# Transformer block with two attentions: the output weights and the feed forward's second weights at another place in SBUF, the attended values too

## What is computed

```python
h = layernorm(x, ln1);  x = attention(h, h, sa_wq, sa_wk, sa_wv, sa_wo) + sa_bo + x
h = layernorm(x, ln2);  x = attention(h, ctx, ca_wq, ca_wk, ca_wv, ca_wo) + ca_bo + x
h = layernorm(x, ln3);  p = h @ ff_w1 + ff_b1
a, gate = p[..., :1024], p[..., 1024:]
out = (a * gelu(gate)) @ ff_w2 + ff_b2 + x
```

## The kernel before, in words

| tile | byte | modulo 512 | modulo 1024 |
|---|---|---|---|
| `w_hi`, all four slots | 16512 | 128 | 128 |
| `w_lo`, all four slots | 49280 | 128 | 128 |
| `hT_hi` | 133184 | 64 | 64 |
| `hT_lo` | 137280 | 64 | 64 |
| `qk_hi`, `qk_lo`, `v_f` | 141376, 149568, 157760 | 64 | 64 |
| `pT` | 190720 | 256 | 256 |
| `a_hi` | 207168 | 320 | 320 |
| `a_lo` | 215360 | 320 | 320 |

## Time and profile before

### The profile page before, as it was taken

How to read it: one execution, slowest core, us unless ns; L and a number is a source line. 1 busy time by engine, 2 the same in 40 slices (tenths; PEclk the granted TensorE clock), 3 DMA queues, 4 the chain that set the end, 5 groups by cost and what they waited for, 6 DMA issues and landing times.

```text
span 2864.2 us, 72446 instructions
## 1 busy us (share of the span) xinstructions
PE 2842.0 (99%) x25278; PEld 2485.3 (87%) x25278; DVE 2256.3 (79%) x3495; ACT 1912.3 (67%) x6041; POOL 1471.1 (51%) x1310
## 2 busy tenths in 40 slices
PE   8999999999999999999999999999999999999999
PEld 6888888888888888888888888888888889999999
DVE  6888888888888888888888888888888865555554
ACT  6677766677766776777777777777777754444443
POOL 5444444444444444765555555555555544554554
PEclk9999999999999999999999999999999999999999
DMA  5666666666666666667777776666766632222222
GB/s 147 158 162 157 156 157 159 158 154 145 151 151 154 150 148 149 161 166 177 177 172 169 173 171 169 168 164 165 168 168 163 151 100 88 73 73 84 81 73 63
DMA packets 355360, 413.32 MB, mean 144 GB/s; under 512 B 122048, under 2 KB 209472, under 8 KB 355264
## 3 DMA queue, kind: packets, MB, share of 16 engines
q1 hardware_dynamic: 345120, 395.29, 57.4%
q10 hardware_dynamic: 10144, 16.78, 1.6%
HBM read 94.52 MB, written 49.02 MB: 50 GB/s over the span
## 4 chain that ended last, share of the span: by engine, by line
PE 98%; DVE 1%; ACT 1%; POOL 0%; issue 0%; DMA 0%; DVEq 0%; POOLq 0%; ACTq 0%
PE unit_ps L593 54%; PE o_ps L618 17%; PE s_ps L606 14%; PE s_ps L593 12%; DVE neg_max L1021 0%; ACT probs L851 0%; DVE blocks L1035 0%; POOL probs L1253 0%; DMA x_ln<-in_x_dram 0%; ACT qk_hi L882 0%; DVE qk_lo L1046 0%; DVE hT L1016 0%; DVE hT_lo L1059 0%; ACT x_n L828 0%; ACT L828 0%
## 5 line engine op out<-in xcount | busy, mean ns | idle before, releaser
L1253 POOL TENSOR_TENSOR probs<-probs,row_inv 128x1024 f32<-128x1024 f32 x512 | 967.8, 1896 | 893.9 <-DVE row_inv L1026 893.9
L851 ACT ACTIVATE probs<-s_ps,neg_max 128x256 f32<-128x256 f32 x2048 | 950.4, 487 | 403.9 <-DVE neg_max L1021 403.4
L1021 DVE TENSOR_REDUCE neg_max<-s_ps 128x4 f32<-128x1024 f32 x512 | 616.8, 1205 | 62.8 <-PE s_ps L606 58.4
L1035 DVE STREAM_TRANSPOSE blocks<-probs 128x1024 f32<-128x1024 f32 x512 | 633.2, 1237 | 19.9 <-POOL probs L1253 19.9
L593 PE MATMUL unit_ps<-hT_hi,w_hi 128*128 128x256 f32 x2048 | 571.3, 282 | 3.0 <-DVE hT_lo L1059 2.6
L593 PE MATMUL unit_ps<-hT_hi,w_lo 128*128 128x256 f32 x2048 | 554.0, 277 | 0.0
L618 PE MATMUL o_ps<-pT,v_f 128*64 128x256 f32 x4096 | 498.5, 385 | 1.7 <-DVE a_lo L1041 1.7
L593 PE MATMUL unit_ps<-hT_lo,w_hi 128*128 128x256 f32 x1792 | 496.1, 277 | 0.0
L851 ACT ACTIVATION_READ_ACCUMULATOR probs<-s_ps,neg_max 128x1 f32 x2048 | 444.6, 217 | 0.0
L593 PE MATMUL unit_ps<-w_hi,a_hi 128*128 128x256 f32 x1536 | 430.8, 280 | 3.8 <-DVE a_lo L1041 2.8
L593 PE MATMUL unit_ps<-w_lo,a_hi 128*128 128x256 f32 x1536 | 425.7, 277 | 0.0
(11 more groups left out here) (73 smaller groups left out, 6017.8 us busy)
## 6 DMA issues: line engine op xcount, KB each, us to landing
pT<-blocks SPq DMA_DIRECT2D x1024, 256.0 KB, 4.5
rows_t_dram<-row_blocks SPq DMA_DIRECT2D x91, 256.0 KB, 4.4
rows_in<-rows_t_dram SPq DMA_DIRECT2D x91, 256.0 KB, 4.1
x_res<-in_x_dram SPq DMA_DIRECT2D x32, 256.0 KB, 4.1
x_sa_dram<-x_out SPq DMA_DIRECT2D x32, 256.0 KB, 4.3
x_ln<-x_sa_dram ACTq DMA_DIRECT2D x32, 256.0 KB, 4.9
ctx_in<-in_ctx_dram SPq DMA_DIRECT2D x32, 256.0 KB, 4.4
x_res<-x_sa_dram SPq DMA_DIRECT2D x32, 256.0 KB, 4.1
```

The costliest lines, as they stand in the source:

```text
L851: op = nc.scalar.activation(probs[:, m % 2, r, :].rearrange("p (j b c) -> p j b c", j=IT, c=BLK), scored.rearrange("p (j c b) -> p j b c", ...
L1021: nc.vector.tensor_reduce(neg_max[:, m % RING, :], s_ps[:, m % 2, :, :].rearrange("p h (i j) -> p (h i) j", j=S), AX_X, ALU.max, negate=Tr ...
L1035: nc.vector.transpose(blocks[:, n % 2, :, m % 2, :].rearrange("p b (j r c) -> p r j b c", j=IT, c=BLK), probs[:, m % 2, :, :].rearrange("p ...
L1253: nc.gpsimd.tensor_tensor(probs[:, m % 2, :, :], probs[:, m % 2, :, :], row_inv[:, m % RING, :].unsqueeze(2).broadcast_to([P, ROWS, S]), A ...
```

## The change

The fourth slot of the weights (`streamed`) is put 64 bytes further than its neighbours, and 448 bytes behind it make each of the two weight tiles 33280 bytes long, 65 times 512. The 64 bytes ahead of the attended values go. `ff_w2` now lives in the fourth slot, where `wo` was; its raw form is loaded to slot 2 of the staging as before. Since `wo` is in use to the end of the attention, the split is made in two halves: each half waits until `wo`'s same half is used for the last time (`at.wo_full`).

```diff
+        def weights(name):
+            loaded = sb(f"{name}_loaded", [P, 3, WCOLS], F32R)
+            sb(f"{name}_between", [P, 16])
+            streamed = sb(f"{name}_streamed", [P, WCOLS], F32R)
+            sb(f"{name}_behind", [P, 112])
+            return [loaded[:, i, :] for i in range(3)] + [streamed[:]]
+
+        w_hi, w_lo = weights("w_hi"), weights("w_lo")
...
-        sb("before_attended", [P, 16])
         a_hi = sb("a_hi", [P, PAIRS, S], F32R)
         a_lo = sb("a_lo", [P, PAIRS, S], F32R)
-        sb("behind_attended", [P, 16])
...
+        def down_half(half):
+            return slice(half * WCOLS // 2, (half + 1) * WCOLS // 2)
...
                     last = product(bank[:, 0:D], three(a_hi[:, m, rows], a_lo[:, m, rows],
-                                                       w_hi[:, 2, m * D:(m + 1) * D], w_lo[:, 2, m * D:(m + 1) * D]),
+                                                       w_hi[3][:, m * D:(m + 1) * D], w_lo[3][:, m * D:(m + 1) * D]),
...
+                            if d == FT // 2 and parts == START:
+                                pe.wait_ge(ff_w2_lo, 2)
                             down(t, d)
...
+            def split_down_weight(half):
+                act.wait_ge(at.wo_full, 2 * TOTAL - 1 + half)
+                if half == 0:
+                    act.wait_ge(ff_ld[2], 16 * 4)
+                cols = down_half(half)
+                nc.scalar.activation(w_hi[3][:, cols], w_stage[2][:, cols], ACT.Copy).then_inc(ff_hi_done, 1)
...
-                split_ff_weight(2)
+                split_down_weight(0)
...
+                    if m == BEGUN and parts == START:
+                        split_down_weight(1)
...
+            def split_down_weight(half):
+                pool.wait_ge(ff_hi_done, 3 + half)
+                cols = down_half(half)
+                nc.gpsimd.tensor_tensor(w_lo[3][:, cols], w_stage[2][:, cols], f32(w_hi[3][:, cols]), ALU.subtract).then_inc(ff_w2_lo, 1)
...
-                pool.wait_ge(ff_hi_done, 3)
-                nc.gpsimd.tensor_tensor(w_lo[:, 2, :], w_stage[:, 2, :], f32(w_hi[:, 2, :]), ALU.subtract).then_inc(ff_w2_lo, 1)
+                split_down_weight(0)
...
+                    if m == BEGUN and parts == START:
+                        split_down_weight(1)
                     if "cur" in parts:
                         hidden_lo(t, m)
```

More of the change, by code:

```diff
@@ L185, in block_kernel @@
         o_ps = psum("o_ps", [P, 2, S])
-        w_hi = sb("w_hi", [P, 4, WCOLS], F32R)
-        w_lo = sb("w_lo", [P, 4, WCOLS], F32R)
-        w_stage = sb("w_stage", [P, STAGES, WCOLS])
+        def weights(name):
[5 more added lines that the diff above has]
+        w_hi, w_lo = weights("w_hi"), weights("w_lo")
+        w_raw = sb("w_raw", [P, STAGES, WCOLS])
+        w_stage = [w_raw[:, i, :] for i in range(STAGES)]
         ln_gain = sb("ln_gain", [P, 3, DK])
@@ L470, in load_cross_weight @@
                     rows = PAIRS // 4
-                    sp.dma_start(w_stage[:, slot, cols].rearrange("p (k n) -> p k n", k=rows),
+                    sp.dma_start(w_stage[slot][:, cols].rearrange("p (k n) -> p k n", k=rows),
                                  w.rearrange("(k p) n -> p k n", p=P)[:, quarter * rows:(quarter + 1) * rows, :]).then_inc(ca_ld, 16)
@@ L486, in load_ff_weight @@
                     rows = w.shape[1] // 4
[L487 removed]
+                    sp.dma_start(w_stage[k][:, cols].rearrange("p (k n) -> p k n", k=rows),
                                  w[:, quarter * rows:(quarter + 1) * rows, :]).then_inc(ff_ld[k], 16)
                 else:
[L490 removed]
+                    sp.dma_start(w_stage[k][:, cols], w[:, cols]).then_inc(ff_ld[k], 16)
             def in_register(value):
@@ L627, in projection @@
                     if side == 1 and k == DK - 1:
-                        terms += [(w_hi[:, slot, w], hT_hi[:, side, k, tokens]), (w_lo[:, slot, w], hT_hi[:, side, k, tokens])]
+                        terms += [(w_hi[slot][:, w], hT_hi[:, side, k, tokens]), (w_lo[slot][:, w], hT_hi[:, side, k, tokens])]
                     else:
-                        terms += three(w_hi[:, slot, w], w_lo[:, slot, w], hT_hi[:, side, k, tokens], hT_lo[:, side, k, tokens])
+                        terms += three(w_hi[slot][:, w], w_lo[slot][:, w], hT_hi[:, side, k, tokens], hT_lo[:, side, k, tokens])
                 return terms
@@ L645, in project_out @@
                                [term for m in range(half * HALF, (half + 1) * HALF)
-                                for term in three(a_hi[:, m, rows], a_lo[:, m, rows], w_hi[:, 3, m * D:(m + 1) * D],
-                                                  w_lo[:, 3, m * D:(m + 1) * D])])
+                                for term in three(a_hi[:, m, rows], a_lo[:, m, rows], w_hi[3][:, m * D:(m + 1) * D],
+                                                  w_lo[3][:, m * D:(m + 1) * D])])
                 if it == IT - 1:
@@ L694, in hidden @@
                     last = product(s_ps[:, m % 4 // 2, m % 2, half * S:(half + 1) * S],
-                                   [term for k in range(DK) for term in three(w_hi[:, k, cols], w_lo[:, k, cols],
+                                   [term for k in range(DK) for term in three(w_hi[k][:, cols], w_lo[k][:, cols],
                                                                               hT_hi[:, parity, k, :], hT_lo[:, parity, k, :])])
@@ L986, in split_ff_weight @@
                 dve.wait_ge(ff_hi_done, k + 1)
-                nc.vector.tensor_tensor(w_lo[:, k, :], w_stage[:, k, :], f32(w_hi[:, k, :]), ALU.subtract).then_inc(ff_lo_done, 1)
+                nc.vector.tensor_tensor(w_lo[k], w_stage[k], f32(w_hi[k]), ALU.subtract).then_inc(ff_lo_done, 1)
             def norm_statistics(ph, b):
```

12 lines of the change are left out of this document (6 added, 6 removed).

## The result

| | before | after |
|---|---|---|
| median of 4 runs each, same chip | 2865.86 us (2864.95 to 2867.11) | 2886.99 us (2885.99 to 2889.31) |
| ratio, 95% interval | | 1.0073 [1.0059, 1.0087] |
| the profiled execution's own time | 2866.01 us | 2889.31 us |
| its span | 2864.2 us | 2887.5 us |

The change makes the kernel 21 us slower, where 7 us less were predicted; 2887 lies outside the range of 2851 to 2872.

The account below looks back on a forecast made before the run. TensorE's matmul pace was taken as the bound. Gains of 10.2 and 1.5 us less 4.6 for crossings, all else 0, took the profiled 2866.0 to 2858.9, the median to 2858 us; range 2851 to 2872.

Parts of the forecast that it names:

- What bounds the kernel: Whole kernel: TensorE busy 99% of the span, no wait worth removing, so the pace between matmuls of one shape decides.
- The slow pair is the one of odd m: Steady feed forward: hidden and down units of odd m run at 118.3 ns a matmul, the others at 113.9.
- Term 1: Operand places: output and down products at distance 64 turn quick; 10.2 and 1.5 us won, 4.6 given back, net 7.1.
- Its charge for crossings, 18 ns each: Between down and next hidden unit, distance -64 plus settling costs 18 ns at 256 crossings, 4.6 us.
- Modulo 512: All operand places: the distance, stationary less moving, was counted modulo 512 bytes, giving 64, 192 and -64.
- Term 2: v units: w_lo moves by 512 bytes, expected cost 0; 1 ns either way on 1408 matmuls would be 1.4 us.
- Term 3: Split of the down weights in two halves at the turn: all covered, by 1.4 us at the tightest, cost 0.
- Places don't matter: Rival for the paces: destination bank or 512 bytes decide, 2865.2 us; chance 0.28 including only down and output products mending, 2860.3.
- quick without giving back: Rival at the crossings: they cost nothing and v gains some ns; 2853.5 us, or 2851; chance 0.13.
- The slower rival: Qk and even hidden units: w_lo moved by 512 modulo 1024 keeps them slow; +21, 2886 us; chance 0.14.
- Two read ports: TensorE: the skill's rule of independent ports, making places irrelevant, was doubted over an alternation of 4.4 ns a matmul.

Follow-up runs that it names:

- e3: The kernel before, with 512 bytes of padding behind the high and 512 behind the low weights, so only w_lo moves modulo 1024; 2865.12 us, ratio 0.9999.
- e12: All weights at 128 as before, attended values moved to 448: distances 128 at entry, 64 within, 0 on the way out; 2877.74 us, ratio 1.0041 to before.
- e9: Changed kernel with e1's wait, streamed weights at 320, attended values at 384: distance 64 at entry, within and way out; 2853.72 us, ratio 0.9968 to before.
- e1: The changed kernel, but GpSimd's first half of the split waits until VectorE has written hT_lo; 2887.13 us, ratio 1.0074 to before.
- e7: Changed kernel with e1's wait, streamed weights at 384 (128 modulo 256, as before), attended values at 320; 2865.4 us, ratio 1.0000 to before.
- e5: From e1, streamed weights left at 192 as in the change, attended values back at 320; 2891.36 us, ratio 1.0091 to before.
- e6: From e1, streamed weights back at 128, attended values left at 256 as in the change; 2885.76 us, ratio 1.0070 to before.
- e8: Changed kernel with e1's wait, streamed weights at 64, attended values at 320: distance 0 within modulo 256; 2897.68 us, ratio 1.0113 to before.
- e13: e9 with one more padding ahead of all tiles, every place 64 bytes further and all distances unchanged; 2852.92 us, ratio 0.9953 to before.
- e10: Changed kernel with e1's wait, streamed weights at 256, attended values at 320: distances 0 at entry, 64 within, 128 out; 2885.03 us, ratio 1.0069 to before.
- e11: Changed kernel with e1's wait, streamed weights at 192, attended values at 384: distances 64 at entry, 192 within, 192 out; 2882.00 us, ratio 1.0065 to before.

## Why the prediction was wrong, point by point

**What bounds the kernel: right.** TensorE's pace of issue, read from starts and chain and not from durations, decides: every difference in the table of stretches but those of the start and the turn is a difference of spacing without a wait.

**"The slow pair is the one of odd m": a correlation, taken for a cause.** e3 has a slow m = 4 and a quick m = 5 at the turn. The flip at the way out was in the earlier trace rows to be read: the pace that enters a hidden unit there is not the one that leaves it. I had written that down unit hands the pace on and then looked for the cause in m.

**Term 1, "distance 64 leads from slow to quick; distance 192 keeps what it was given": this is the step that failed.** It was read from the earlier trace rows, where a hidden unit settles in three matmuls. But that unit had been entered at distance 0 out of 192; the settling belonged to the crossing and not to the 64 behind it. With 64 within and 192 at both crossings an output unit is slow and stays slow through 24 matmuls (after), a hidden unit through its 12, and so are the output units with 128 ahead (e12). With 64 at all three places, once slow, the units of e9 stay slow for its last 25 us. A gain of 10.2 us less 4.6 was credited where the feed forward lost 7.5. Distances alone don't say it all here either: at the turn of e1, with the distances of after, m = 4 and m = 5 do become quick after five matmuls (1.38 us each), and are slow again from m = 6 on.

**Its charge for crossings, 18 ns each, was of the wrong kind.** A crossing is not a price paid once: it sets the pace of the whole unit behind it. At 118 ns against 113.5, 23 spacings of an output unit cost 0.104 us more (2.918 against 2.814).

**The largest item was missing.** The `wo` units behind qk units were quick before. They entered the sum only where they were slow, as 1.5 us to be won; that a new crossing could take away the pace of the quick ones had no line, and that, with the qk units behind the scores' output products, was 13 us. The one exception in after went as predicted: behind the scores of the cross attention the first 12 settle (221, 120, 117, 116, then 113 and 114 ns), 1.48 us where it was 1.52, which makes 1.2 of the 1.5 us; but the 22 qk matmuls behind them then go slow, 2.59 instead of 2.51.

**Modulo 512: wrong.** e7 shows 256. With 256 the distances I called 64 and 192 were still two different ones, so this did not make the error.

**Term 2, the v units at 0: right.** Their 1408 matmuls take 350.6 us of starts against 351.7, and the difference is one unit at 36 us, in the stretch where before has the lower clock; all units behind the first four take 343.46 against 343.44 us.

**Term 3, the split at 0: right for the median, wrong for the profiled execution.** The second halves disturbed nobody: GpSimd's began at 2349.98 in after, in the row above, and TensorE did not wait there. What I did not look at is what runs beside the first half: GpSimd's and VectorE's instructions with both operands in SBUF. And I took the 4.33 us of the output product for its length, though 24 such matmuls take 2.96 in the same rows; it was at the low clock, and at full clock it releases the copy over a microsecond sooner. `hT_lo` went from 0.69 to 2.83 us (+2.1), and TensorE came out of the wait at a lower clock (+1.5). The Trainium skill (SBUF — State Buffer, Who interferes with whom) says that a VectorE instruction with two SBUF inputs contends with a GpSimd instruction that reads SBUF; the trace agrees, with 2.83 us beside GpSimd and 0.69 without it.

**The rivals.** "Places don't matter" is refuted by after and by e5, e6 and e8 to e12; "quick without giving back" held in after only for the 12 output matmuls behind the scores, and would have been right for e9: its bound of 2853.5 us, all units quick, is what e9 measured (2853.72) and e13 (2852.92). The slower rival gave 2886 and the result is 2887, but its mechanism, `w_lo` at 512 modulo 1024, moves nothing in e3; qk units behind scores stayed at 2.838 us in after. The number was luck.

**Two read ports.** e8 and e9, which differ by nothing but paddings, are 44 us apart at the same count of matmuls. The Trainium skill (TensorE: Matmul & The Clock Gate, Step-by-step: what each phase is for) says that loading the next weights takes no read bandwidth from the running matmul; by that rule they would be alike. That the two operands meet in SBUF is the natural reading of a dependence on their distance alone, and it stays an inference: no run here separates the weight load from the matmul.

**What stays open.** The mechanism behind 256 bytes; why 128 has a cycle of six and 0 a constant 120 ns; why each crossing keeps or flips as it does (the table is an observation, not a rule that would foretell a new layout, as e10 and e12 show); why the same distances can hold either pace, and what starts a slip; why the low clock at the start lasts longer in some executions; what e9's two long executions were, and why e11's four fell into two groups (2876.6 twice, 2887.4 and 2888.8).

## What to carry to other kernels

In a stream of short matmuls where nobody waits, take the spacing of starts unit by unit, and list for each boundary of units whether it keeps or loses the pace; a unit that is quick now is as much at stake as one that is slow. Copy, for new operands, all the distances of a sequence that keeps its pace (here 64 modulo 256 at the entry, within and at the way out), and measure any other combination before believing it. Look at the whole length of the trace too: e9 kept the quick pace through 454 us of steady feed forward, lost it to one matmul that came 40 ns late, and did not find it again. When work is moved to GpSimd or split, look at which VectorE instruction with two SBUF operands will run beside it, above all if TensorE waits for that one.

## What was not expected of the hardware

Matmuls of 256 columns in fp32r, at full clock and without a wait, come at 113.3 ns, 118 or 120 ns. Which of them goes by the distance of their operands' places modulo 256 bytes, at the crossing and within, and by the pace that they come from: 44 us of 2865 between e9 and e8. The state is kept for 24 matmuls and more, in both directions, with the same distance of operands within: 64 at 113.3 ns (e9) and at 118 (after, and e9 behind its slip), 192 at 113.5 (before, behind qk units) and at 118 (e11). The profile's busy share does not show it: TensorE is busy 100% of the steady feed forward at 3993 matmuls and at 4143. The same VectorE instruction takes 2.83 us beside a GpSimd instruction and 0.69 us without it.
